# Value product of an attention in two column halves per key tile, and a causal mask laid on the exponentials by GpSimd

## The reference

```python
def attention(x, Wqkv, Wproj, bproj):              # L3; L1 is the same without the mask
    qkv = (x @ Wqkv).reshape(b, t, 3, H, hd).transpose(2, 0, 3, 1, 4)
    q, k, v = (qkv[0], qkv[1], qkv[2])
    scores = jnp.einsum('bhqd,bhkd->bhqk', q, k) * hd ** (-0.5)
    scores = jnp.where(jnp.tril(jnp.ones((t, t), bool)), scores, -jnp.inf)
    attn = jax.nn.softmax(scores, axis=-1)
    out = jnp.einsum('bhqk,bhkd->bhqd', attn, v)
    return out.transpose(0, 2, 1, 3).reshape(b, t, c) @ Wproj + bproj
...
x = x + gate * attention(layernorm(x) * (1 + scale) + shift, ...)
h = gelu((layernorm(x) * (1 + scale_mlp) + shift_mlp) @ W1 + b1)
x = x + gate_mlp * (h @ W2 + b2)
```

## Time and profile before

| | |
|---|---|
| three runs, median (lowest to highest) | 497.06 us (495.15 to 497.51) |
| the profiled execution | 498.7 us, its span 496.6 us |
| mean granted TensorE clock | 0.931 of full speed |
| busy: TensorE, VectorE, ScalarE, GpSimd | 65%, 63%, 49%, 22% |
| non-causal attention, slots 0 to 63 | about 198 to 301 us |
| causal attention, slots 0 to 63 | about 378 to 473 us |

### The profile page before, as it was taken

How to read it: one execution, slowest core, us unless ns; L and a number is a source line. 1 busy time by engine, 2 the same in 40 slices (tenths; PEclk the granted TensorE clock), 3 DMA queues, 4 the chain that set the end, 5 groups by cost and what they waited for, 6 DMA issues and landing times.

```text
span 496.6 us, 6007 instructions
## 1 busy us (share of the span) xinstructions
PE 321.8 (65%) x2017; PEld 151.0 (30%) x2018; DVE 311.0 (63%) x787; ACT 242.7 (49%) x422; POOL 108.4 (22%) x160
## 2 busy tenths in 40 slices
PE   0025845621346463877777888867758999999886
PEld 0014523410115320121111224543412333334454
DVE  0778787859688568778888723335666555565230
ACT  3267556552564221466666685342422445555542
POOL 0112149632262510000000040173300000000410
PEclk9999999999999966599999999997965999999899
DMA  7940440000000332000000000000360000000001
GB/s 251 416 165 0 170 176 0 1 0 0 1 0 1 97 94 64 2 0 2 1 3 1 3 2 0 1 0 0 86 170 1 3 2 2 2 2 3 2 1 42
DMA packets 11650, 21.90 MB, mean 44 GB/s; under 512 B 2010, under 2 KB 10462, under 8 KB 10846
## 3 DMA queue, kind: packets, MB, share of 16 engines
q1 hardware_dynamic: 11620, 21.52, 12.6%
HBM read 14.57 MB, written 0.52 MB: 30 GB/s over the span
## 4 chain that ended last, share of the span: by engine, by line
PE 46%; DVE 26%; ACT 11%; issue 8%; POOL 6%; DMA 2%; SPq 0%; DVEq 0%; ACTq 0%; POOLq 0%
PE ps L1455 11%; PE ps L1437 7%; DVE nm L918 7%; PE pe L1477 4%; PE pe L1358 4%; PE ps L1510 4%; PE ps L1442 3%; POOL rstd L341 2%; PE pe L1480 2%; ACT scr L1130 2%; PE ps L1412 2%; DVE st L500 2%; ACT scr L1042 2%; PE ps L1229 1%; DMA big<-in_wa 1%
## 5 line engine op out<-in xcount | busy, mean ns | idle before, releaser
L918 DVE TENSOR_REDUCE nm<-ps 128x1 f32<-128x512 f32 (+2 forms) x224 | 135.0, 648 | 55.8 <-PE ps L1442 34.7
L1155 ACT ACTIVATE scr<-pe 128x1024 f32<-128x1024 f32 (+3 forms) x128 | 108.9, 866 | 102.5 <-PE pe L1480 59.2
L1437 PE MATMUL ps<-big 62*128 62x512 bf16 (+3 forms) x256 | 50.5, 386 | 36.3 <-DVE nm L918 32.6
L1455 PE MATMUL ps<-scr 128*32 128x512 f32 (+3 forms) x512 | 61.3, 552 | 6.2 <-ACT scr L1130 5.4
L341 POOL TENSOR_TENSOR rstd<-var,half 128x4 f32<-128x4 f32 x26 | 28.5, 1098 | 114.2 <-DVE var L505 88.2
L1477 PE MATMUL pe<-big 64*128 64x512 bf16 (+3 forms) x256 | 47.2, 367 | 1.1 <-ACT scr L1155 1.1
L425 POOL CAST nm<-nm 128x16 bf16<-128x16 f32 x16 | 3.2, 198 | 196.7 <-DVE nm L918 196.7
L1437 PEld LDWEIGHTS ps<-big 62*128 62x128 bf16 x256 | 14.5, 96 | 65.9 <-DVE nm L918 49.3
L1477 PEld LDWEIGHTS pe<-big 64*128 64x128 bf16 x256 | 12.5, 95 | 53.3 <-issue 24.9
L1358 PE MATMUL pe<-hT,w 128*128 128x512 f32 x48 | 24.6, 638 | 3.5 <-ACT hT L1109 3.5
L510 DVE TENSOR_SCALAR xn<-x_tok,mv,rstd 128x128 f32<-128x128 f32 x56 | 15.8, 344 | 13.6 <-POOL rstd L341 13.5
(11 more groups left out here) (221 smaller groups left out, 592.9 us busy)
## 6 DMA issues: line engine op xcount, KB each, us to landing
big<-tern SPq DMA_DIRECT2D x48, 128.0 KB, 2.4
big<-in_fill SPq DMA_DIRECT2D x1, 4096.0 KB, 13.6
big<-in_wa SPq DMA_DIRECT2D x1, 2304.0 KB, 12.5
w<-in_w SPq DMA_DIRECT2D x2, 1152.0 KB, 19.3
big<-in_wa SPq DMA_DIRECT2D x1, 1344.0 KB, 6.2
big<-in_w SPq DMA_DIRECT2D x1, 1024.0 KB, 14.3
w<-in_w SPq DMA_DIRECT2D x1, 896.0 KB, 20.0
rowg<-in_rowg SPq DMA_DIRECT2D x1, 832.0 KB, 18.3
```

The source lines that it names most:

```text
L918: v.tensor_reduce(dst, src[:, 0:w * len(pairs)].rearrange("p (h w) -> p h w", w=w), AX.X, ALU.max, negate=True).then_inc(sem(f"a{a}_max"), 1)
L1155: s_.activation(P[:, kt % 2, 2 * p:2 * p + 2, q0:S], E[(e - 1) % 2][:, :, q0:S], ACT.Exp, scale=SCALE).then_inc(sem(f"a{a}_p"), 1)
L1437: last = t_.matmul(dsts[par][:, k * wd:(k + 1) * wd], QZ[rows, b, 2 * g + i, qt * 128:(qt + 1) * 128], KZ[rows, b, 2 * g + i, 0:wd], start ...
L1455: last = t_.matmul(bank[6][32 * h:32 * h + 32, q0:S], V[b][:, kt, HG * g + h, :], P[:, kt % 2, h, q0:S], start=(kt == 0), stop=(kt == TB - 1),
```

## The change

- `P` holds four tiles (`PRING`) instead of two, in the upper half of `big`, whose weights are no longer needed then.
- The value product of a key tile is made in two column halves, one per slot. In the non-causal layer tile k's halves stand in slots 2k+3 and 2k+4, in the causal one in 2k+4 and 2k+5 (`LATE`). The first key tile of a unit is done whole in the first of its two slots, and the second has nothing. Two semaphore counts per tile instead of one.
- The mask product of the transposed scores (L1480) is left out. Instead GpSimd sets the upper part of each diagonal block of `P` to zero after the exponential, 128x512 f32 per key tile (`lower_triangle`), and the value product waits for it. The mask of the maxima stays.
- GpSimd's program of an attention follows `schedule` entry by entry: parts and the inverse root at the entry of their ring item, then, at every even entry k from 2 on, the select of tile k/2 - 1, and the bias at entry 58.
- The normalised x of batch element 0 is made by VectorE, behind its statistics, instead of by GpSimd. n_turn stands in slot 59 instead of 60, ScalarE's modulation one exponential earlier.
- The semaphores of the MLPs' hidden tiles are shared by all MLPs and counted on.

```diff
+PRING = 4
...
-        P = scr[:, 0:2 * HG * S].rearrange("p (i h t) -> p i h t", i=2, h=HG)
+        P = wf32[:, NP * B * S:2 * NP * B * S].rearrange("p (i h t) -> p i h t", i=PRING, h=HG)
...
-        EARLY = {52: "o_turn", 54: "proj", 60: "n_turn"}
-        COPIED, MODULATED = 54, 62
+        LATE = (3, 4)
+        EARLY = {52: "o_turn", 54: "proj", 59: "n_turn"}
+        COPIED, MODULATED, BIASED = 54, 61, 58
...
-                        if u == 7:
-                            n_root(n + 1, 0)
-                            pool.wait_ge(sem("n_root"), B * (n + 1) + 1)
-                            for t in tiles(0):
-                                last = nc.gpsimd.tensor_scalar(xn[:, t], x_tok[:, t], mv[:, t, 0:1], rstd[:, t:t + 1],
-                                                               ALU.subtract, ALU.mult)
-                            last.then_inc(sem("n_xn"), 1)
+
+                    def lower_triangle(k):
+
+                        pool.wait_ge(sem(f"a{a}_p"), 2 * (k + 1))
+                        q0 = 128 * (k % TB)
+                        block_ = P[:, k % PRING, :, q0:q0 + 128]
+                        nc.gpsimd.affine_select(block_, block_, [[0, HG], [1, 128]], ALU.is_ge, zero, base=0,
+                                                channel_multiplier=-1).then_inc(sem("triangle"), 1)
+
+                    for k, slot in enumerate(schedule(n_max)):
+                        for item, u, *_ in slot:
+                            if item == "parts":
+                                maxima_parts(u)
+                            elif item == "proj" and u == 0:
+                                n_root(n + 1, 0)
+                        if causal and k >= 2 and k % 2 == 0:
+                            lower_triangle(k // 2 - 1)
+                        if k == BIASED:
                             add_bias(n + 1, 0)
...
                             norm_stats(u, NORMS[n + 1][2], "n_var")
+                            if u == 0:
+                                n_normed(n + 1, 0)
...
-                        act.wait_ge(sem(f"a{a}_pv"), TB * (u + 1))
+                        act.wait_ge(sem(f"a{a}_pv"), 2 * TB * (u + 1))
...
-                                if TB * u + kt >= 2:
-                                    act.wait_ge(sem(f"a{a}_pv"), TB * u + kt - 1)
+                                if TB * u + kt >= PRING:
+                                    act.wait_ge(sem(f"a{a}_pv"), 2 * (TB * u + kt - PRING + 1))
...
-                    def probs_out(u, kt):
-
+                    def probs_out(k, part):
+
+                        u, kt = k // TB, k % TB
                         b, g = u // 4, u % 4
                         q0 = 128 * kt if causal else 0
-                        pe.wait_ge(sem(f"a{a}_p"), 2 * (TB * u + kt + 1))
-                        if kt == 0 and u >= 1:
-                            pe.wait_ge(sem(f"a{a}_pvs"), u)
+                        mid = (q0 + S) // 2
+                        lo, hi = (q0, S if kt == 0 else mid) if part == 0 else (mid, S)
+                        if kt == 0 and part == 1:
+                            return
+                        if part == 0:
+                            if causal:
+                                pe.wait_ge(sem("triangle"), k + 1)
+                            else:
+                                pe.wait_ge(sem(f"a{a}_p"), 2 * (k + 1))
+                            if kt == 0 and u >= 1:
+                                pe.wait_ge(sem(f"a{a}_pvs"), u)
                         for h in range(HG):
-                            last = t_.matmul(bank[6][32 * h:32 * h + 32, q0:S], V[b][:, kt, HG * g + h, :],
-                                             P[:, kt % 2, h, q0:S], start=(kt == 0), stop=(kt == TB - 1),
+                            last = t_.matmul(bank[6][32 * h:32 * h + 32, lo:hi], V[b][:, kt, HG * g + h, :],
+                                             P[:, k % PRING, h, lo:hi], start=(kt == 0), stop=(kt == TB - 1 and part == 1),
                                              tile_position=(0, 32 * h))
-                        last.then_inc(sem(f"a{a}_pv"), 1)
+                        last.then_inc(sem(f"a{a}_pv"), 2 if kt == 0 else 1)
...
-                                             QZ[rows, b, 2 * g + p, q0:S], start=True, stop=not causal)
-                        for j in range(2 * causal):
-                            last = t_.matmul(E[s % 2][:, j, q0:q0 + 128], cmask[:, 0], cmask[:, 2], start=False, stop=True)
+                                             QZ[rows, b, 2 * g + p, q0:S], start=True, stop=True)
                         last.then_inc(sem(f"a{a}_sc"), 1)
                         for x in slots[s + 1]:
                             ring_item(*x)
-                        if p == 1 and s > 1:
-                            probs_out((s - 2) // 8, (s - 2) // 2 % 4)
-                    probs_out(7, TB - 1)
+                        if s >= LATE[causal]:
+                            probs_out((s - LATE[causal]) // 2, (s - LATE[causal]) % 2)
+                    for half_ in range(64 - LATE[causal], 64):
+                        probs_out(half_ // 2, half_ % 2)
```

More of the change, by code:

```diff
@@ L97, in build @@
         ident = sb("ident", [128, 128])
-        cmask = sb("cmask", [128, 3, 128], BF16)
+        cmask = sb("cmask", [128, 2, 128], BF16)
         inv = sb("inv", [128, 11])
@@ L229, in build @@
         LAG = 1
-        EARLY = {52: "o_turn", 54: "proj", 60: "n_turn"}
-        COPIED, MODULATED = 54, 62
+        LATE = (3, 4)
+        EARLY = {52: "o_turn", 54: "proj", 59: "n_turn"}
+        COPIED, MODULATED, BIASED = 54, 61, 58
         TURNS = [(n, b) for n, _, _ in SEQ for b in range(B) if b or n not in (1, 5)]
         MLP_NO = {n: i for i, n in enumerate(MLPS)}
+        HIDDENS = {n: B * sum(MLPS[k]["n"] for k in MLPS if k < n) for n in MLPS}
         TURN_BANK, QK_BANKS, V_BANKS = 4, (2, 3, 6, 2), (5, 3)
@@ L337, in _ @@
             link = chained(pool, "pool_chain")
+            zero = pool.to_reg(0.0)
             def inv_root(dst, src, wait, count, done, n):
@@ L419, in _, with maxima_parts @@
                     a = 0 if layer == 1 else 1
-                    n_max = len(max_steps(layer == 3))
-                    for u in range(8):
+                    causal = layer == 3
+                    n_max = len(max_steps(causal))
+                    def maxima_parts(u):
                         m = nm[:, u % 2].rearrange("p (r k) -> p r k", r=2)
@@ L897, in _ @@
                             if item == "norm":
-                                dve.wait_ge(sem("n_xn"), B * (n + 1) + 1)
                                 n_normed(n + 1, u)
@@ L1152, in _ @@
                                 act.wait_ge(sem(f"a{a}_sc"), e)
-                                if TB * u + kt >= 2:
-                                    act.wait_ge(sem(f"a{a}_pv"), TB * u + kt - 1)
-                                s_.activation(P[:, kt % 2, 2 * p:2 * p + 2, q0:S], E[(e - 1) % 2][:, :, q0:S], ACT.Exp,
+                                if TB * u + kt >= PRING:
+                                    act.wait_ge(sem(f"a{a}_pv"), 2 * (TB * u + kt - PRING + 1))
+                                s_.activation(P[:, kt % PRING, 2 * p:2 * p + 2, q0:S], E[(e - 1) % 2][:, :, q0:S], ACT.Exp,
                                               scale=SCALE).then_inc(sem(f"a{a}_p"), 1)
@@ L1166, in _ @@
                             i = m["n"] * b + c
-                            act.wait_ge(sem(f"n{n}_h"), i + 1)
+                            act.wait_ge(sem("n_h"), HIDDENS[n] + i + 1)
                             s_.activation(hid[:, b, c], bank[2 + i % 4], m["func"],
-                                          bias=col[:, m["bias"] + c:m["bias"] + c + 1]).then_inc(sem(f"n{n}_hid"), 1)
+                                          bias=col[:, m["bias"] + c:m["bias"] + c + 1]).then_inc(sem("n_hid"), 1)
                     if n + 1 in MLPS and MLPS[n + 1]["func"] != m["func"]:
@@ L1356, in mlp_in @@
                 if i >= 4:
-                    pe.wait_ge(sem(f"n{n}_hid"), i - 3)
+                    pe.wait_ge(sem("n_hid"), HIDDENS[n] + i - 3)
                 t_.matmul(bank[2 + i % 4], m["w"][:, m["at"] + c * D:m["at"] + (c + 1) * D], hT[:, b],
-                          start=True, stop=True).then_inc(sem(f"n{n}_h"), 1)
+                          start=True, stop=True).then_inc(sem("n_h"), 1)
             for n, kind, layer in SEQ:
@@ L1506, in _ @@
                             turn_1()
-                        pe.wait_ge(sem(f"n{n}_hid"), m["n"] * (b + 1))
+                        pe.wait_ge(sem("n_hid"), HIDDENS[n] + m["n"] * (b + 1))
                         for i in range(TB):
@@ L1559 @@
     i = np.arange(128)
-    cmask = np.stack([np.eye(128), np.where(i[None] > i[:, None], NEG, 0.0), np.where(i[:, None] > i[None], NEG, 0.0)], 1)
+    cmask = np.stack([np.eye(128), np.where(i[None] > i[:, None], NEG, 0.0)], 1)
     sel = np.zeros((2, B, 128), np.float32)
```

## The result

| | before | changed |
|---|---|---|
| median of 5 runs (lowest to highest) | 496.94 us (495.15 to 497.51) | 501.31 us (499.71 to 502.1) |
| ratio, with its 95% interval | 1 | 1.0091 (1.0062 to 1.012) |
| span of the profiled execution | 496.6 us | 500.4 us |

A forecast was written before the change was run, and what follows sets the result against it. No engine over 65% busy, so order decides: VectorE's maxima pace the non-causal layer, TensorE bounds the causal. -5.7 + 8.65 + 1.5 = +4.4 us on the 497.06 median gives 501.5 us; range 493 to 511.

The forecast's parts named there:

- The term was -5.7: Non-causal layer: halves close VectorE's gaps (4.4 us, 0.8 more at the low clock), moved normalisation 0.5; bounds 0 and -10.
- The wait at the parts: Causal layer: TensorE stands 1.5+D a unit because the casts for the parts queue behind a select awaiting a late exponential.
- D: Duration of one GpSimd select over 128x512 f32 per causal key tile, taken as 1.4 us, bounds 0.53 and 3.2.
- the sum: Whole-kernel change as a function of D, 8.45 D - 7.4: -2.9 us at 0.53, zero at 0.87, +22 at 3.2.
- rival 3: Causal select with D between 0.57 and 1.17 us: gains and waits cancel, about 497.5 us; chance 0.20.
- rival 2: Causal select cheap, below 0.57 us, so the non-causal gain decides: 494.2 us; chance 0.25.
- Rival 4: TensorE's clock falls in the causal wait at the parts, 1.5 us a unit, 509 us; or D near 2.5, 511; chance 0.17.
- The forecast's own case: Causal layer's parts held behind the select: 501.5 us, own range 499.6 to 506, D from 1.17 to 2; chance 0.38.
- three signs of being wrong: Selects well under 1 us, an exponential of slot 8u+3 done before the copy, or a clock that falls.
- Five units, forecast 8.65: Causal layer, slots 11 to 51: unit period 12.15 + D, or 13.55 us against 11.82, so +8.65 us over five units.
- The last stretch, forecast +1.5: End of the causal layer: root, bias and late selects delay the last copy, +1.5 us; -1.5 at D = 0.53, +10.5 at 3.2.
- The first eleven slots, forecast even: Causal layer's first unit: masks less halving save 1.3 us and somewhat more, against some 2 us waited at the first parts.

The follow-up runs named there:

- e3: Against the changed kernel: halves in both layers, causal value halves one slot earlier, TensorE mask product back, no select; 490.25 us, 0.9873 of before.
- e2: Against the changed kernel: causal layer gets whole value products in slot 2k+3 and TensorE's mask product back, no select; 489.94 us, 0.9864 of before.
- e1: Changed kernel, but in the causal layer GpSimd makes the parts of slot 8u+4 ahead of the select of tile 4u+1; 485.02 us, 0.9767 of before.
- e5: Changed kernel with every causal-layer select made twice, the second changing nothing; 510.66 us, 1.0276 of before.
- e4: Changed kernel with 14 unread products put into TensorE's wait ahead of the parts of causal units 2 to 6; 494.11 us, 0.9948 of before.
- e7: e1 with the first half of tile 4u+1 ahead of the third maxima step in the causal layer's slots 8u+6; 483.28 us, 0.9737 of before.
- e9: e2 with batch element 0's normalised x made by GpSimd again, n_turn in slot 60, modulation one exponential later; 490.38 us, 0.9877 of before.

## Why the prediction was right, and which of its terms were not

**Non-causal layer: mechanism right, size short.** Gaps of 0.26 gone, 0.61 kept (0.52), unit 11.74 against a forecast 11.9. The term was -5.7, the profile shows -8.7: 3.0 us lie ahead of the first copy, 4.9 in the five units from there to unit 5's copy (12.73 to 11.74 each), 0.8 behind it. Granted clock in windows of 2 us, before, then changed:

```profile
206.00:208.00 2.00, 1.76 (x11) 0.30 (x7) 0.89 (x2) 1.22 (x2) 0.29 (x2) 0.50 0.00 0
...
212.00:214.00 2.00, 1.56 (x12) 0.29 (x10) 1.98 (x4) 1.53 (x2) 0.00 (x0) 0.76 0.00 0
```

```profile
204.00:206.00 2.00, 1.82 (x11) 0.30 (x7) 0.84 (x2) 0.87 (x1) 0.61 (x3) 0.85 0.00 0
206.00:208.00 2.00, 1.15 (x12) 0.38 (x12) 1.56 (x5) 1.07 (x2) 0.00 (x0) 1.00 0.00 0
```

The clock rose near 213 us before and near 204.6 us after. In e3 it rose at 212.5 us again, and this first stretch (first exponential to first copy) took 18.65 us there, 19.53 before and 16.5 to 17.0 in the other runs above. So the estimate of 0.8 us for the first halves fits e3, and some 2 us more are the moment at which the clock rises, which varies between executions of kernels that are the same up to there. They are no part of the change's worth: e2, with this layer alone changed, gains 6.3 us over several runs, near the forecast's 5.7.

**Causal layer, place and chain: right.** The wait at the parts was to be 1.5+D with the select's D; with D = 0.635 that is 2.1, measured 2.05. e1 takes it down to 0.61 us by the order alone, and e5 lengthens it by 0.70 us with a second select of 0.634.

**D: wrong by a factor of two.** The step that failed is "I take D = 1.4, nearer to the row of the same size". 0.635 us lies near the lower bound, the memset of 0.526; the one row of this shape that reads a tensor was a tensor_tensor, and it misled. The Trainium skill (GPSIMD Engine Reference, section 7) has 1.03 cycles an element for an unrolled compare-and-select body, an estimated 0.44 us for 512 elements at 1.2 GHz plus the dispatch, and 2.03 for one that is not. The measured 0.635 us lies between the two estimates of 0.45 and 0.9 us in the prediction. At D = 0.635 the sum gave -2.0 us, a time of 495: D lies on rival 3's ground, the time near rival 2's 494.2. (The sum is not quite linear: 8.45 D - 7.4 gives 19.6 at D = 3.2, where the parts give 22.)

**The clock: the rival that came true beside the forecast.** Rival 4 priced the clock's fall at 1.5 us a unit and 7.5 in all; e4 shows 1.56 and 7.8. The forecast's own case left it out. So the total came out right by luck: the D that was 0.77 us too long stood in for the clock that fell. Two of the prediction's own three signs of being wrong came true, selects well under 1 us and a clock that falls; with D as measured and the clock as priced, its own sum is about 502.5 us. Five units, forecast 8.65: the smaller D takes 3.8 off; the period at the full clock is 12.24 and not 12.15 + 0.635 = 12.79, which takes another 2.8 off; the clock adds 7.8: 9.86 as measured. In the period, the wait ahead of the third step was 0.81 for 0.9 [e1's row at 403.38]; the rest of the 0.55 lies in TensorE's work, which I had as 9.5 us and which is nearer 9.1: scores without a mask behind them are followed by the next maxima product sooner (in e4 after 0.12 us for 256 columns and 0.22 for 512, where before the change the mask product started 0.21 and 0.32 behind the scores).

**The ends.** The last stretch, forecast +1.5 with D = 1.4 and -1.1 with 0.635, measured +1.0: the clock was low there for 6.8 us, before for 3.4. The first eleven slots, forecast even, took 18.6 us against 16.8; the clock rose 15.3 us after the first exponential, before the change after 8.0. In e7 it rose after 8.8 us and the stretch took 15.8 us, in e1 after 15.0 us and 18.1, although e7's edit is worth 0.46 us a unit elsewhere. So much of the 1.8 us goes with the clock, but how much, and why it rises later, stays open. The 0.5 us for the normalised x measured 0.1 in e9.

**What follows for the change.** Its three parts have three signs. Halves pay in the non-causal layer (e2) and cost 0.44 us a unit in the causal one (e3). The select is worth 0.9 us a unit against the mask product (10.90 against 11.82, halving included), as long as the parts are not queued behind it.

## What to carry to other kernels

When work is given to an engine that has room, place it in that engine's queue by what stands behind it, not by when its own input usually comes: here an item of 0.64 us with a late input held up three casts of 0.2 us, and TensorE with them. Price a wait of TensorE by itself and by the clock that it may cost, as two terms; filling the wait with dummy products separates them in one run. A product split in halves pays where another engine's cadence is broken by the whole one, and costs its fixed 0.15 us where TensorE is the bound.

## What the runs showed of the hardware that was not expected

- A GpSimd affine_select over 128x512 f32, in place, takes 0.635 us, half of a tensor_tensor of that shape (1.268) and hardly more than a tensor_scalar over a quarter of it (0.603).
- Behind TensorE's wait of about 2.05 us in each of the five units of the causal layer the granted clock fell to 0.50, three times for 3.4 us and twice for 6.8; the same unit with 1.69 us of products in the wait, or with a wait of 0.6 us and another of 0.8, stayed at 1.0.
- Five runs of the changed kernel had a mean granted clock of 0.81 four times and 0.91 once (500.34 us, within the others' 499.7 to 502.1). The profiled one was low from about 63 to 205 us (slices 6 to 16 of the page, with short stretches at full clock), mostly ahead of the first attention, and that cost no time that can be seen: in the six traces with such a low stretch the first exponential comes at 197.3 to 198.4 us, in the five without at 197.3 to 198.8.
